# Groups of four sequences instead of pairs, with the feed-forward inside the attention slots

## The reference

```python
x = x + attn0(layernorm(x))       # 16 heads of 16 features, softmax with a maximum
                                  # for each block of 256 keys; no bias
x = x + ffn0(layernorm(x))        # ternary 256 -> 1024, plus a gated term of rank 16,
                                  # relu, square, ternary 1024 -> 256
x = x + attn1(layernorm(x))       # 16 heads, softmax over all 512 keys, biases
x = x + ffn1(layernorm(x))        # 8 trees of 255 nodes: silu(logits) where the node
                                  # lies on the path that the decisions take, 2040 -> 256
```

## Time and profile before

| | |
|---|---|
| runs | 3227.5, 3227.98, 3229.15 us; median 3227.98 |
| the profiled execution | 3225.8 us from first to last instruction |
| PE busy | 3042.1 us (94%), 20635 products |
| PE weight loads | 1396.6 us (43%) |
| DVE busy | 2215.8 us (69%) |
| ACT busy | 1923.5 us (60%) |
| POOL busy | 944.8 us (29%) |
| granted clock of TensorE | 0.991 of full on average |

### The profile page before, as it was taken

One profiled execution on the slowest core, in us unless ns is written; L12 is line 12 of the kernel. 1 busy time (PEld: TensorE's weight loads), 2 busy tenths in 40 slices (PEclk: granted clock), 3 DMA queues, 4 the chain that ended last, 5 costly groups with the idle time before them and its releaser, 6 DMA issues.

```text
span 3225.8 us, 51764 instructions
## 1 busy us (share of the span) xinstructions
PE 3042.1 (94%) x20635; PEld 1396.6 (43%) x20635; DVE 2215.8 (69%) x4090; ACT 1923.5 (60%) x2567; POOL 944.8 (29%) x1215
## 2 busy tenths in 40 slices
PE   5999999999999999999999999999999999999999
PEld 2243552435534255343643436434364343634336
DVE  7858568585675856768576675767757676676764
ACT  4746548475483754738557484574745657465574
POOL 4132231422314133141321413214142141422413
PEclk7999999999999999999999999999999999999999
DMA  4000000000000001000110001000010000100000
GB/s 146 23 21 22 28 34 23 20 23 27 34 23 21 22 27 42 14 21 23 37 35 12 21 22 43 28 12 31 12 52 27 5 31 21 45 28 2 31 19 21
DMA packets 92735, 91.10 MB, mean 28 GB/s; under 512 B 15787, under 2 KB 89907, under 8 KB 92483
## 3 DMA queue, kind: packets, MB, share of 16 engines
q1 hardware_dynamic: 92495, 87.79, 8.0%
HBM read 17.48 MB, written 8.39 MB: 8 GB/s over the span
## 4 chain that ended last, share of the span: by engine, by line
PE 64%; DVE 26%; ACT 5%; issue 2%; POOL 1%; SPq 1%; DMA 0%; DVEq 0%; POOLq 0%
PE ps L1036 13%; PE ps L1081 11%; PE ps L1106 11%; PE ps L1323 9%; DVE nmax L758 8%; DVE nmax L761 8%; PE ps L1042 5%; PE ps L1061 4%; PE ps L1294 3%; PE ps L1092 3%; ACT probs L555 3%; DVE hT L744 1%; PE ps L1049 1%; PE ps L1129 1%; PE ps L1314 1%
## 5 line engine op out<-in xcount | busy, mean ns | idle before, releaser
L555 ACT ACTIVATE probs<-ps 128x1024 f32<-128x1024 f32 x1024 | 1042.3, 1025 | 359.8 <-PE ps L1092 354.4
L1081 PE MATMUL ps<-kst,qst 48*128 48x512 f16 x2048 | 703.3, 388 | 114.8 <-DVE nmax L758 53.3
L758 DVE TENSOR_REDUCE nmax<-ps 128x2 f32<-128x512 f32 x1024 | 650.2, 684 | 168.2 <-PE ps L1081 163.3
L761 DVE TENSOR_REDUCE nmax<-ps 128x1 f32<-128x512 f32 x1024 | 650.1, 684 | 165.5 <-PE ps L1081 162.1
L1092 PE MATMUL ps<-qst,kst 54*128 54x512 f16 x2048 | 682.0, 385 | 5.0 <-ACT probs L555 5.0
L1106 PE MATMUL ps<-probs,vn 128*32 128x512 f32 (+1 forms) x5184 | 572.8, 515 | 6.6 <-ACT oT L541 6.6
L1081 PEld LDWEIGHTS ps<-kst,qst 48*128 48x128 f16 x2048 | 164.3, 93 | 719.8 <-DVE nmax L758 309.0
L449 POOL TENSOR_TENSOR probs<-probs 127x512 f16<-127x512 f32 (+1 forms) x256 | 292.4, 1164 | 519.5 <-ACT probs L708 519.5
L708 ACT ACTIVATE probs<-probs 127x512 f16<-127x512 f32 (+1 forms) x256 | 161.3, 630 | 350.3 <-DVE probs L1012 346.7
L1323 PE MATMUL ps<-wout,probs 127*128 127x256 f16 (+1 forms) x3072 | 357.2, 273 | 0.0
L1036 PE MATMUL ps<-hT,win 128*127 128x512 f16 (+1 forms) x1536 | 354.3, 380 | 2.7 <-ACT probs L684 2.7
(11 more groups left out here) (121 smaller groups left out, 3334.0 us busy)
## 6 DMA issues: line engine op xcount, KB each, us to landing
qst<-parts SPq DMA_DIRECT2D x384, 64.0 KB, 2.6
kst<-parts SPq DMA_DIRECT2D x384, 64.0 KB, 2.6
x<-in_x SPq DMA_DIRECT2D x16, 512.0 KB, 3.9
probs<-x SPq DMA_DIRECT2D x16, 512.0 KB, 3.0
out<-probs SPq DMA_DIRECT2D x16, 512.0 KB, 3.0
qst<-nrow SPq DMA_DIRECT2D x256, 12.0 KB
probs<-in_winT SPq DMA_DIRECT2D x1, 2040.0 KB, 8.7
probs<-in_wfcT SPq DMA_DIRECT2D x1, 1024.0 KB, 7.0
```

The lines of the kernel that those rows point to most:

```text
L555: nc.scalar.activation(probs[:, g % 2, 2 * hf:2 * hf + 2, s % G, :], ps[:, 2 + 2 * hf:4 + 2 * hf, :], ACT.Exp).then_inc(exp_rd, 1)
L758: nc.vector.tensor_reduce(nmax[:, u, 2 * tt + half, :, slot], bank[tt % 2].rearrange("p (a s) -> p a s", s=BLK), AX.X, ALU.max, negate=Tru ...
L761: nc.vector.tensor_reduce(nmax[:, u, 2 * tt + half, 0, slot:slot + 1], bank[tt % 2], AX.X, ALU.max, negate=True).then_inc(max_rd, 1)
L1081: mm(bank[tt % 2], qst[lo:hi, ai % 2, e // 2, tt * P:(tt + 1) * P], kst[lo:hi, ai % 2, e // 2, :], start=True, stop=True).then_inc(max_ps, 1)
```

## The change

The group is now four sequences, so there are four groups instead of eight pairs. A group has eight attention slots, which are all written by one function `attention(b, i)` per engine (slots 0 to 3 are layer 0, 4 to 7 layer 1), and then 32 trees. Inside the slots stand:

- `prep` (slots 0 to 6): norm, q, k and v of the next slot's sequence.
- `post` (slots 1 to 7): from weighted values to residual of the slot before.
- `ffn` (slots 2 to 5): the whole feed-forward of one sequence (eight `hidden` units, four `ffn_out` units; each `ffn_out` sums one tile of tokens over all eight units at the end).
- `after` (slots 1 to 4 and 7): the norm that the feed-forward, or the first eight trees, need.

The separate feed-forward stage is gone, and all calls of `keep_going` with it but for nine products at the end of the tree stage. The units stand in two places of a head: between the third and the fourth pair of tiles, and behind the fourth.

PSUM: score tiles have banks 2, 3 and 4. Of each three tiles in a row the first two share one `exp` of 1024 columns, the third has one of 512. Bank 5 takes the weighted values, and banks 6 and 7 all units. `homes()` gives each tile of exponentials one of 20 places in SBUF, which is reused as soon as the values' product that read it is over. All low halves of the squares are on POOL (half were on DVE), with two buffers where there were four. The weighted values are never cut in halves. x is kept in place through the trees, so the copy `probs<-x` is gone.

```diff
-PAIR = 2
-PAIRS = B // PAIR
+QUAD = 4
+QUADS = B // QUAD
...
-            def exps(b, ph, s, hf):
...
-                nc.scalar.activation(probs[:, g % 2, 2 * hf:2 * hf + 2, s % G, :],
-                                     ps[:, 2 + 2 * hf:4 + 2 * hf, :], ACT.Exp).then_inc(exp_rd, 1)
+            def exps(b, i, s, kt):
+                tile = i * TILES + s * T + kt
+                if tile % 3 == 0:
+                    return
+                act.wait_ge(exp_ps, b * EXPS + exp_after(tile))
+                free = max(free_after(tile), free_after(tile - 1) if tile % 3 == 1 else 0)
+                if free:
+                    act.wait_ge(pv_step, b * (PHASES * H) + free)
+                if tile % 3 == 2:
+                    at = home_of(tile)
+                    nc.scalar.activation(pr[:, at, :], bank[4], ACT.Exp).then_inc(exp_rd, 1)
+                else:
+                    lo, hi = sorted((home_of(tile - 1), home_of(tile)))
+                    nc.scalar.activation(pr[:, lo:hi + 1:hi - lo, :], ps[:, 2:4, :], ACT.Exp).then_inc(exp_rd, 1)
...
+            def scores(b, i, s, kt):
+                n, tile = b * PHASES + i, i * TILES + s * T + kt
+                if tile >= 3 and tile % 3 != 1:
+                    pe.wait_ge(exp_rd, b * EXPS + exp_after(tile - 3))
...
+            def square(f, c):
+                pool.wait_ge(relu_rd, f * M0 + (c + 1))
+                if c >= 2:
+                    pool.wait_ge(sq_lo, f * M0 + (c - 1))
+                nc.gpsimd.tensor_tensor(r2[:, c % 2, :], rr[:, c % 2, :], rr[:, c % 2, :], ALU.mult).then_inc(sq, 1)
...
+            def attention(b, i):
+                n = b * PHASES + i
+                post, prep, ffn = i > 0, i + 1 < PHASES, 2 <= i < 2 + QUAD
...
+                    for kt in (0, 1):
+                        if ahead:
+                            maxima(*ahead, kt)
+                        scores(b, i, s, kt)
+                    if s >= G:
+                        weighted(n, s // G - 1, s % G)
+                    elif post:
+                        weighted(n - 1, NG - 1, s)
+                    if ahead:
+                        maxima(*ahead, 2)
+                    scores(b, i, s, 2)
...
+                    if (s, 0) in HID and ffn:
+                        c = HID[s, 0]
...
+                        hidden(b, q, c)
...
+                    if ahead:
+                        maxima(*ahead, 3)
+                    scores(b, i, s, 3)
```

More of the change, by code:

```diff
@@ new lines, in _ @@
+                send(b, 2)
+                if more:
+                    stack_up(n8, 2)
+                    stack_up(n8, 3)
+                    replace(b, 2)
+                    rows_up(n8, 0)
+                send(b, 3)
+                if more:
+                    replace(b, 3)
+            for q in range(QUAD):
+                sp.wait_ge(y_out[q], 16 * QUADS)
+            for q in range(QUAD):
+                sp.wait_ge(x_in[q], 16 * QUADS)
+            for q in range(2):
+                sp.wait_ge(stack[q], (16 * 4 * SLOTS) * (QUADS * PHASES))
+                sp.wait_ge(mstack[q], 64 * QUADS * PHASES)
@@ new lines, in _ @@
+            for b in range(QUADS):
+                more = b + 1 < QUADS
+                for i in range(PHASES):
+                    attention(b, i)
+                n8 = (b + 1) * PHASES
+                for a in range(TREES):
+                    if a % PAR == 5 and a < TREES - PAR:
+                        rstd_of(b, f"T{a // PAR + 1}")
+                    if more and a == 22:
+                        rstd_of(b + 1, "A0")
+                    if more and a == 25:
+                        qk_low(n8, 0)
+                        qk_low(n8, 1)
+                    if more and a == 27:
+                        qk_low(n8, 2)
+                        qk_low(n8, 3)
@@ new lines, in attention @@
+                    if s == 9 and post:
+                        natural(n - 1, 3, 6)
+                    if s == 12 and post:
+                        attn_residual(n - 1, 0, 7)
+                    if s == 13 and after:
+                        if after == "T0":
+                            for half in range(2):
+                                after_attention(n - 3, half)
+                        else:
+                            after_attention(n - 1, 1)
+                        moments(b, after)
@@ new lines, in attention @@
+                    if ahead:
+                        maxima(*ahead, (3,))
+                    if s == 2 and prep:
+                        hT_low(b, nxt, 0, 6)
+                    if s in (10, 11) and post:
+                        attn_low(n - 1, s - 10, POST_T, 7)
+                    if s == 12 and after and after != "T0":
+                        after_attention(n - 1, 0)
+                    if s == 14 and after:
+                        normalise(b, after)
+                    if s == 15 and after:
+                        hT_low(b, after, 0, 7)
+                        hT_low(b, after, 1, 6)
@@ L915, in _ @@
             for e in range(4, LEAD):
-                maxima(0, 0, e, range(T))
+                maxima(0, e, range(T))
             dve.wait_ge(attn_in, 16 * len(other_loads))
@@ new lines, in weighted @@
+            def weighted(n, g, kt):
+                b, tile = n // PHASES, n % PHASES * TILES + (g * G + G - 1) * T + kt
+                if kt == 0 and n + g:
+                    pe.wait_ge(oT_sb, n * NG + g)
+                if kt == 0 and g == 0:
+                    pe.wait_ge(v_sb, n * 2 + 2)
+                pe.wait_ge(exp_rd, b * EXPS + exp_after(tile))
+                for j in range(G):
+                    a = G * g + j
+                    at = kt * H * VW + a * VW
+                    i = mm(bank[5][32 * j:32 * j + 32], vn[:, n % 2, at:at + 2 * HD], pr[:, HOME[n % PHASES * NG + g, j, kt][0], :],
+                           start=kt == 0, stop=kt == T - 1, skip_group_check=True)
+                i.then_inc(pv_step, 1)
@@ new lines, in _, with lead_tiles @@
+            for b in range(QUADS):
+                more = b + 1 < QUADS
+                for i in range(PHASES):
+                    if b == 0 and i == 1:
+                        pe.wait_ge(w_lo_pool, POOLED)
+                    attention(b, i)
+                n7, n8 = b * PHASES + PHASES - 1, (b + 1) * PHASES
+                def lead_tiles(i):
+                    e, tt = lead[i]
+                    maxima(n8, e, tt)
+                    maxima(n8, e, tt + 1)
+                weighted(n7, NG - 1, 0)
+                pe.wait_ge(exp_rd, (b + 1) * EXPS)
@@ L1544, in bits @@
+            pe.wait_ge(tree_upd, QUADS * (2 * QUAD))
 def bits(c):
```

1495 lines of the change are left out of this document (660 added, 835 removed).

## The result

The changed kernel is slower: 3292.99 us in the median of three runs (3286.24 to 3298.93) against 3227.98, ratio 1.0195 with the interval [1.0171, 1.0219]. The forecast was 3075. The profiled execution has a span of 3284.5 us.

The account below looks back on a forecast made before the run. Attention slots were taken as bound by DVE and PE's wait for a free maxima bank, feed-forward and trees by PE; 78.4 + 4 x 752.5 - 18.1 + 4 = 3074 us, stated as 3075 in the runs' measure, range 2950 to 3190.

Parts of the forecast that it names:

- Set-up, trees, transfers, the feed-forward's PE work: Set-up 78.4 us, tree stage 220, transfers taken at 0, PE's work in a feed-forward slot 70.7 us.
- the forecast's 75: A feed-forward slot with second norm: PE's 70.7 us, 1.3 for DVE and 3.2 for ring, about 75 us.
- The ring: Three score banks in attention heads: waits for the wide exponential cost 0.2 us a head, bounds 0 and 0.63.
- The rival on its far side (3330): Ring and evictions bind: ACT's ordered waits add up, a head loses 0.5 us; 3330 us, slower, chance 0.10.
- The sign that the forecast gave: In feed-forward slots, score tiles' wait for the exponential replaces the maxima's waits as PE's largest.
- Its own warning: Forecast is wrong if feed-forward slots pass 85 us, or slots without feed-forward are over 65.
- The clock at 1.00 but for short falls at slot starts: Expected sign for PE's granted clock: full speed, with only short falls where slots start.
- a rival: The clock falls without fillers at starts of slots 0, 1, 6, 7: 32 x 1.7 = 54 us, 3130, chance 0.12.
- I add 5 us a group: DVE's norm passes slowed beside POOL's squares: eleven passes, half hit by 0.9 us; bounds 0 and 14.
- in heads 0, 1 and 15 ... DVE is longer, by 1.3 in all: Feed-forward slots are PE's, except these heads where a norm pass beside four maxima makes DVE longer, 1.3 us.
- Slots 0, 1 and 6: Slots without feed-forward, sized from like stages of the kernel before: 56, 63 and 61 us.
- the 3 for the ring: Slot 0: 3 us for the ring added to the earlier layer-1 even slot's 52.8, giving 56.

Follow-up runs that it names:

- kernel of 3178 us: Changed kernel with POOL's wait for the normalisation, fillers in sparse heads of slots 0, 1, 6, and the second v unit in bank 6: 3177.94 us, ratio 0.9836.
- The one wait of POOL: Changed kernel; in slots 2 to 5 GpSimd waits for the four normalisations' end before going on with squares: 3220.92 us, ratio 0.9966.
- The run with short low halves: 3178 us kernel with VectorE writing 32 of 512 columns of feed-forward norms' low halves (15 of 16 norms), output not the reference's: 3166.78 us, ratio 0.98.
- The second v unit's wait for the rows' copy: Changed kernel with POOL's wait and fillers, plus second v unit into bank 6 in slots 0, 1, 6, 7: 3177.94 us, against 3191.68 without.
- the units behind the fourth pair: 3178 us kernel with the units of a head's first place moved behind its fourth pair of tiles: 3178.23 us, ratio 0.9837.
- the ring in the kernel before: Kernel before with three score banks, exponentials over 1024 and 512 columns in turn, score-bank fillers sent to bank 5: 3348.82 us, ratio 1.0372.

## Why the prediction was wrong

The forecast was 218 us too low. Edits to the changed kernel give back 115 of them, the larger part with its cause shown. The other 103 are found by place below, with only a part of them tested.

*Set-up, trees, transfers, the feed-forward's PE work.* Right to a few us. The first scores come at 82.9 us, where 78.4 were forecast and 81.4 was before (the 3 us gain of the set-up didn't come). The trees are 221.2. PE's waits put down to transfers are 5 us in all in the changed kernel and 11 in that of 3178 us. Heads 3 to 15 of a feed-forward slot take 62.6 to 63.7 us at full clock in the kernel of 3178 us, where the forecast's 75 less some 13 for heads 0 to 2 (an estimate from its own terms) leave 62. The products by line of fillers are 27.

*The ring.* Right as far as tested: 0.17 us a head alone in the kernel before where 0.2 was taken; in the changed kernel it was not measured by itself. The rival on its far side (3330), which ended slower, had the right sign for the wrong reason: score tiles wait for exponentials 28 us in all. The sign that the forecast gave, the score tiles' wait in place of the maxima's as PE's largest, didn't come either: behind the set-up PE waited 197 us for maxima, where it was 70 before. Its own warning did: slots 0, 1 and 6 are over 65 us, while the feed-forward slots stay under 85.

*Step that failed first: "The clock at 1.00 but for short falls at slot starts".* The forecast knew the mechanism, put it at nothing in its sum, and gave it as a rival a chance of 0.12 and 54 us, from one fall of 3.41 us and 1.7 us of work. The sum over rows shows where that number broke. The third group has 34 us of (1 - clock) x length, not 8 x 1.7 = 14, since a fall lasted up to 17 us in stretches where PE still had gaps. Two runs price it from both sides: fillers taken from the kernel before cost 45 us, fillers put into the sparse slots of the changed one give 45. Further falls, some 20 us, hung on the gap of head 2, which is the next step.

*Step that failed second: "I add 5 us a group", for DVE beside POOL, bounds 0 and 14.* One place alone, head 2 of the four feed-forward slots, costs 2.0 to 2.3 us a slot directly (3.83 to 6.15 at full clock), about 9 a group and within the bounds. What the term left out is what stands behind it: in 11 of 16 slots the clock fell in the gap, and head 2 was 7.6 (seven times) or 8.6 us (four times) instead of 6.15, some 20 us in all. The one wait of POOL was worth 52 us in the feed-forward slots and 72 in all, where the forecast had 20 for the whole kernel. Its 0.9 us a pass was also read against a mean (4 x 0.42) that itself holds passes beside GpSimd: alone, four take 1.38 us in the kernel before, so the 2.62 of the earlier trace rows was 1.2 over it, and 3.70 in this place is 2.3 over it. The forecast had treated a longer DVE instruction and a fall of the clock as two cases with chances of their own; they are one chain.

By the Trainium skill ("GPSIMD Engine Reference", section 1 Specifications) GpSimd shares its SBUF interfaces with VectorE, and they contend where the VectorE instruction has two SBUF inputs or runs in a 2-port mode. Whether a normalisation runs in such a mode no trace says. The traces agree with what the forecast took from it: the normalisations went from 1.38 to 3.70 us for four, and the maxima, which read PSUM, stay at 684 and 685 ns in the mean before and after. In the changed kernel 253 maxima lie almost wholly beside a long GpSimd instruction and take 685 ns, as do the 1462 beside none.

*Third: "in heads 0, 1 and 15 ... DVE is longer, by 1.3 in all".* With the clock at 1.00 and POOL waiting, the four feed-forward slots are 313.3 us for 298, 3.8 a slot, most of it in heads 0 to 2 (15.1 to 15.4 us for about 13, the estimate from above). The run with short low halves shows DVE as the bound in heads 0 and 1. I had counted maxima and the norm pass's long instructions, and not the seven small ones between them nor PE's waits for one of the two maxima banks (1.0, 1.0 and 0.3 us in heads 0, 1 and 2 of one such slot); the parts of these 3.8 us beyond the low halves' 1.1 were not separated by a run.

*Slots 0, 1 and 6.* 62.2, 65.3 and 68.2 for 56, 63 and 61 in the kernel of 3178 us. A part is a slip in the sum: the 63 is 52.8 + 6.5 + 4 and leaves out the 3 for the ring that slot 0 has, and the 61 is worked out from it. With the ring they are 66 and 64, 6 us a group more and 24 in all. Its fillers are 68 products a group, 14.6 us at 0.215, beside and partly in these 15.7; how much of it is theirs no run separates. Without them the clock takes more: with POOL's wait alone the three slots of the third group are 206.9 us, and with the fillers beside it 198.4. The second v unit's wait for the rows' copy (14 us in all by its run) was in no term.

The books for the kernel of 3178 us: a group is 777.4 for 752.5, the 24.9 being 15.3 (feed-forward slots) + 15.7 (slots 0, 1, 6) - 2.2 (slot 7) + 1.1 (trees) - 5 (the term for POOL, no longer due). Four groups are 100 of the 103 us to 3075. This is a sum by place and not by cause. The other 115 us up to 3293 are POOL's wait and the fillers, 101 together, and the v unit's 14.

## What to carry to other kernels

A product that keeps PE going is not to be booked at its length: the fillers here had 122 us of products and were worth 45 us of time, since they lay behind DVE or held the clock. Before taking such work out, look for the heads in which another engine binds, add up (1 - clock) x length in a run without it, and don't size a fall by the shortest one seen. When two engines share a way, look at what is queued behind the slowed instruction: one wait on the engine with time to spare made the kernel 72 us faster. And when an edit leaves the total as it was, read it by slot: the units behind the fourth pair gained 13 us in one kind of slot and lost 13 in another.

## What the runs showed of the hardware that was not expected

- Four normalisations of 256 columns on VectorE take 1.38 us alone and 3.70 us with GpSimd's 512-column instructions beside them. An instruction of 4 columns goes from 0.16 to about 1 us when a GpSimd instruction starts just ahead of it:

```profile
1930.41 1.06 POOL L455 TENSOR_TENSOR arena<-arena 128x512 f32<-128x512 f32 x1 [5.37 <-ACT arena L612]
1930.48 1.01 DVE L785 TENSOR_TENSOR dif<-stats 128x4 f32<-128x4 f32 x1
1931.41 0.15 DVE L786 TENSOR_TENSOR vpe<-stats 128x4 f32<-128x4 f32 x1
```

- A stretch at half clock lasted 3.41 us with PE busy all through it, and 17.05 us at the start of slot 0 with PE busy 14.49 of them. In the kernel of 3178 us, with fillers in slots 0, 1 and 6, none of the eight behind the set-up is longer than 3.41. That PE's gaps make the length is argued from these; no run varied them alone.
- Falls differ from one group to the next of the same program (head 2 of the same slot: 6.15, 7.6 or 8.6 us), and the times scatter: 3335.98 to 3370.67 for the ring in the kernel before, 3286.24 to 3298.93 for the changed kernel, 3175.67 to 3180.45 for the fastest. The number of falls alone does not order them: the first has 14 in its profiled execution, the second 33.
